# A scan with routing on one Trainium2 core: GpSimd's waits for the residual and for dt move one product ahead, and the token numbers come from a table

## The reference

```python
x_ssm, x_gate = split(x @ in_proj_w.T + in_proj_b)
x_conv = silu(causal_conv4(x_ssm) + conv_b)
Bm, Cm = split(x_conv @ bc_w.T + bc_b)            # 16 states
dt = softplus(x_conv @ dt_w.T + dt_b)
h = h * exp(dt * A) + dt * Bm * x_conv            # step by step over 512 tokens
y = (sum_n h * Cm + x_conv * D) * silu(x_gate)
x = norm(x + (norm(y @ out_w.T + out_b + x) * ln_g + ln_b))
top4 = the 4 best of 8 experts by x @ router_w.T + router_bias, softmax weights
x = norm(x + sum over top4 of weight * expert(x))
```

## Time and profile before

| | |
|---|---|
| time, median of 3 runs | 1290.69 us (1286.31 to 1291.71) |
| time of the profiled execution | 1288.71 us |
| span of the profiled execution | 1286.6 us, so 2.1 us lie around it |
| busy over the span | PE 90%, DVE 82%, ACT 68%, POOL 58% |
| stage 1 | to about 580 us |
| the experts' tiles | from about 580 to 1265 us |
| granted TensorE clock | 0.954 of full speed |

### The profile page before, as it was taken

How to read it: one execution, slowest core, us unless ns; L and a number is a source line. 1 busy time by engine, 2 the same in 40 slices (tenths; PEclk the granted TensorE clock), 3 DMA queues, 4 the chain that set the end, 5 groups by cost and what they waited for, 6 DMA issues and landing times. The chain is left out here.

```text
span 1286.6 us, 17895 instructions
## 1 busy us (share of the span) xinstructions
PE 1153.6 (90%) x5150; PEld 801.9 (62%) x5150; DVE 1053.5 (82%) x1811; ACT 872.4 (68%) x1546; POOL 750.1 (58%) x536
## 2 busy tenths in 40 slices
PE   9879898989898998586979999999999999999960
PEld 4324353535343534255868888888888888888850
DVE  4999999999999999977747777777777777777744
ACT  4675868695959594534647767777677776767745
POOL 0466658888889897976633344433444433444353
PEclk9899999989999998997989999999999999999985
DMA  3543535554545544545856665666665666656638
GB/s 108 213 165 131 182 131 208 175 203 163 195 171 191 187 161 169 212 143 204 283 166 166 156 166 136 160 167 159 167 139 151 166 168 156 155 141 163 166 42 268
DMA packets 69260, 217.21 MB, mean 169 GB/s; under 512 B 7520, under 2 KB 43232, under 8 KB 56288
## 3 DMA queue, kind: packets, MB, share of 16 engines
q1 hardware_dynamic: 33888, 171.61, 37.5%
q0 software_dynamic: 26880, 36.72, 16.5%
q10 hardware_dynamic: 8448, 8.39, 2.0%
HBM read 165.54 MB, written 51.15 MB: 168 GB/s over the span
## 5 line engine op out<-in xcount | busy, mean ns | idle before, releaser
L662 PE MATMUL p_y<-read,small 128*128 128x512 f32 x512 | 252.0, 630 | 54.5 <-POOL read L1312 54.5
L1117 DVE TENSOR_TENSOR_SCAN state<-decay,p_bu 128x512 f32<-128x512 f32 x256 | 297.2, 1202 | 1.7 <-ACT decay L862 1.6
L1640 POOL DMA_INDIRECT total<-o_v,tok x144 | 251.6, 1747 | 39.8 <-issue 39.7
L662 PEld LDWEIGHTS p_y<-read,small 128*128 128x128 f32 x512 | 99.3, 200 | 192.0 <-issue 110.3
L1638 POOL TENSOR_TENSOR scrap<-neg_half 128x1 f32<-128x1 f32 x36 | 22.9, 637 | 314.3 <-ACT o_v L1552 311.8
L520 DVE TENSOR_SCALAR up_v<-up_v 128x512 f32<-128x512 f32 x144 | 69.1, 480 | 144.1 <-ACT up_v L515 139.7
L512 ACT ACTIVATE gate_v<-p_g,bias 128x512 f32<-128x512 f32 x144 | 98.6, 685 | 128.9 <-PE p_up L502 126.8
L862 ACT ACTIVATE decay<-dt,scan_rate 128x511 f32<-128x511 f32 x256 | 162.2, 709 | 10.3 <-DVE state L1117 9.8
L1354 POOL DMA_INDIRECT queues<-rows,index x128 | 129.8, 1014 | 35.0 <-issue 33.0
L1312 POOL TENSOR_TENSOR read<-state,bc 128x1024 f32<-128x1024 f32 x64 | 127.9, 2003 | 37.9 <-DVE p_bu L1108 14.4
L533 ACT ACTIVATE ah<-a_v 128x512 fp32r<-128x512 f32 x144 | 91.3, 634 | 57.9 <-DVE a_v L526 54.8
(11 more groups left out here) (236 smaller groups left out, 2981.5 us busy)
## 6 DMA issues: line engine op xcount, KB each, us to landing
bc<-bc_rows SPq DMA_DIRECT2D x32, 1024.0 KB
first_raw<-in_w_experts SPq DMA_DIRECT2D x19, 1668.0 KB
raw_w<-in_w_experts SPq DMA_DIRECT2D x18, 1668.0 KB
first_wh<-bc_rows SPq DMA_DIRECT2D x16, 1024.0 KB
first_wl<-bc_rows SPq DMA_DIRECT2D x16, 1024.0 KB
first_rows<-queues SPq DMA_DIRECT2D x19, 544.0 KB
xq<-queues SPq DMA_DIRECT2D x18, 544.0 KB
queues<-pad SPq DMA_DIRECT2D x9, 544.0 KB
```

Source lines behind the costliest of these rows:

```text
L662: mm = pe.matmul(p_y[h][:, :], ident[:, :], read[:, t % 4, h, :], start=False, stop=(t == SLOTS - 1))
L1117: dve.tensor_tensor_scan(state[t % 4][:, h, :], decay[(SLOTS * s.n + t) % AHEAD][:, h, :], p_bu[:, h * LEN:(h + 1) * LEN], 0.0, ALU.mult, ...
L1640: pool.indirect_dma_start(total, bass.IndirectOffsetOnAxis(ap=tok[t.p][:, a:a + 1], axis=0), o_v[t.p][:, a, :], None, compute_op=ALU.add). ...
```

## The change

Three things change. (1) POOL's wait for the residual stands ahead of product 7 and not of product 8, its wait for dt ahead of product 11 and not of product 12. (2) The scatters 0 to 6 of a sequence are dealt out anew: 0, 1 and 2 ahead of product 7, 3 ahead of product 9 as before, 4 and 5 ahead of product 11, 6 behind product 14; in round 7 only 0, 1 and 2 move. The second `power` stands ahead of product 11 and not behind it. (3) The constant `token` holds the numbers of all 4096 tokens (32 columns and not 4); ACT copies four columns of it into `rows` ahead of `second_norm`, DVE does so for the last sequence, and the two token steps of `weigh_experts` are gone.

```diff
-    c["token"] = p[:, None] + P * np.arange(TT)[None, :]
+    c["token"] = p[:, None] + P * np.arange(SEQS * TT)[None, :]
...
-                       ("spill", SUBS), ("token", TT), ("ln_g", D), ("ln_b", D), ("b_router", E))
+                       ("spill", SUBS), ("token", SEQS * TT), ("ln_g", D), ("ln_b", D), ("b_router", E))
...
-    ROUTE_STEPS = 12
+    ROUTE_STEPS = 10
...
         def second_norm(r):
             s = r.s.at(-1)
             after(act, s_left, s.n)
+            act.activation(rows[s.p][:, :, COL_TOKEN].bitcast(I32), token[:, TT * s.n:TT * (s.n + 1)], ACT.Copy)
             apply_norm(s, 1, rows[s.p], s_x1)
...
             dve.wait_ge(s_left, s.n)
+            dve.tensor_copy(rows[s.p][:, :, COL_TOKEN].bitcast(I32), token[:, TT * s.n:TT * (s.n + 1)])
             dve.wait_ge(s_last_rstd, 2)
...
-            yield from steps.step(dve.tensor_copy(rows[s.p][:, :, COL_TOKEN].bitcast(I32), token[:, :]))
-            yield from steps.step(dve.tensor_scalar(token[:, :], token[:, :], float(LEN), None, ALU.add))
...
-        BEHIND_READ = (0,)
-        SCATTERS = {9: (1, 2), 10: (3,), 13: (4,)}
-        BEHIND_DRIVE = (5, 6)
-        NEXT_TO_LAST = {9: (1, 2), 10: (3,), 11: (4, 5), 12: (6,)}
+        SCATTERS = {8: (0, 1, 2), 10: (3,), 12: (4, 5)}
+        BEHIND_DRIVE = (6,)
+        NEXT_TO_LAST = {8: (0, 1, 2), 10: (3,), 11: (4, 5), 12: (6,)}
...
-            if r.c and t == 9:
+            if r.c and t == 8:
                 pool.wait_ge(s_residual, r.s.at(-1).n + 1)
-            if r.a and t == 13:
+            if r.a and t == 12:
                 pool.wait_ge(s_dt, r.s.at(1).n + 1)
...
+                if r.c and r.b and t == 12:
+                    power(r.s.at(-1), 1)
                 if r.b:
                     while_scanning(r, t)
...
-                if r.d and r.b and t == 8:
-                    scatter(r.s.at(-2), BEHIND_READ)
...
-                if r.c and r.b and t == 12:
-                    power(r.s.at(-1), 1)
```

## The result

| | before | with the change | ratio, 95% interval |
|---|---|---|---|
| first comparison, median | 1289.7 us | 1277.16 us (1275.62 to 1282.05) | 0.9905 [0.9876, 0.9934] |
| second comparison | 1289.12 us | 1278.31 us | 0.9924 [0.9903, 0.9946] |
| third comparison | 1287.67 us | 1280.18 us | 0.9931 [0.9913, 0.9949] |

The changed kernel is faster by 0.7 to 0.95%. Its first profiled execution is the slowest of the four runs of that comparison, 1282.05 us (span 1280.2); the profiled execution of the second comparison took 1274.84 us (span 1273.0).

The account below looks back on a forecast made before the run. DVE was taken to bound the scans' rounds; 6.55 + 3.1 - 0.5 + 2.35 + 0.3 + 0.85 = 12.65 us off 1288.71 gave 1276.1, set at 1277 us to allow for run scatter; range 1272 to 1283.

Parts of the forecast that it names:

- The residual: DVE's first add of the residual falls to 0.41 us once POOL runs scatters beside it; 6.55 us over rounds 1 to 6.
- dt: `add_log` falls from 1.83 to 1.21 us in rounds 2 to 6; 3.1 us gained.
- The 0.5 taken off for product 10: Deduction because product 10 might still hold `add_log` by up to 0.25 us in the first full rounds.
- Tokens: DVE's two token steps gone: 2.35 us in rounds 2 to 6, 0.3 in round 7, 0.85 behind the scans.
- the sentence that follows product 11 to 347.6: Product 11 ends near 347.6, not 343.5; slot 15's scan needs it at 352, SP's load some 13 us on.
- The rule used for `residual` and `add_log`: A product of POOL holds up a DVE instruction with both inputs in SBUF until the product ends.
- the rule weighed: Whether scatters beside the residual block its add, as the Trainium skill's strict reading says; judged not, nothing charged.
- The prediction's first step: DVE, busy 65.5 of 66.0 us in round 4, sets the pace; shortening its list of a round shortens the round.
- Scatters that hold the adds: Rival: scatters hold the residual and `add_log` as products did; only the tokens' 3.5 us remain, 1285.2 us; chance 0.07.
- PE and ACT as the bound: Rival: PE and ACT set the round, no full round below 66.0 us; gain 6.75 us, 1282 us; chance 0.09.
- The stalled scan: Rival: late product 7 stalls slot 11's scan if POOL pauses between scatters; two pauses give 1301 us; chance 0.04.
- its 0.3: Gain counted in round 7 for the removed token steps, with POOL busy up to the index and through the last product.

## Why the prediction was right, and what in it was not

The time was right: 1277 forecast, medians of 1277.2, 1278.3 and 1280.2 measured, all inside the range. The holds were read rightly, and the scatters freed the adds as said. That the first median lies within 0.2 us of the forecast is luck: single executions of the changed kernel took 1274.84 to 1284.30 us, rounds 1 to 7 gave 8.3 and 9.3 us of the 11.8 that the sum had for them, and what lies ahead of them and behind made up for this or took more away. Point by point:

- *The residual.* 6.55 us forecast, 16.7 - 10.2 = 6.5 measured in the line's busy time. The scatters covered the wait, as said, and the late product 7 did not stall slot 11's scan.
- *dt.* 3.1 us forecast and 3.1 measured. The 0.5 taken off for product 10 was not needed: `add_log` took 1.21 to 1.22 in all rounds, since product 10 ended at 335.9 in round 4 and `add_log` started at 336.16, with 0.25 us to spare.
- *Tokens.* The index follows the weights' step at once. A full round of the change gains 1.84 us and loses 0.21 of `drive`; together that is 2.05 of the forecast 2.09, so the 0.47 is in it. With the tokens alone none of it was. ACT's copy takes 0.19 us.
- *A step that failed* is the sentence that follows product 11 to 347.6 and asks only when slot 15's scan and SP's load need it. Behind product 11 stand products 12 and 13, and in the change they reach the moment when DVE comes to `drive`, which has both inputs in SBUF like the two adds. The rule used for `residual` and `add_log` held for the third such step of the round, and was not asked there. The hold took 0.51 + 1.26 + 0.83 = 2.6 us, nearly all that rounds 1 to 6 lack: 9.25 us against 1.80 + 1.84 + 8.36 = 12.0 without the 0.5. Freeing `drive` gave back 1.5 of it, in rounds 1 and 2; the rest went to `add_log`. A full round was 64.7 us, just outside the forecast 64.4 to 64.6. Some 1.0 of the 1.26 in round 2 come from a cost that the rule weighed left at nothing: it asked whether a scatter holds an add, and not whether an add holds a scatter.
- *The terms do not add as the sum had them.* The prediction's first step, that DVE sets the pace and that what shortens DVE's list of a round shortens the round, fails as long as a step is held. A held step ends when POOL's product ends, and POOL's list from `scale` to `drive` runs without a wait for another engine, from a start that hangs on the gate through PE and ACT: `scale` starts 26.2 us behind the gate of round 4 in before, with the tokens alone and with the residual alone. What DVE saves ahead of a held step is lost in it. Tokens and residual, 8.9 us of the sum over the rounds, gave 0.17% and 0.13% by themselves, with intervals that reach no change, and neither shortened a full round by over 0.1 us. So the sum came out because all parts were made together.
- *Rivals.* Scatters that hold the adds: refuted by the 0.41 us beside two of them. The prediction's evidence for that was thinner than it says, since the compare of 299.07 ran for most of its time in the pause between two scatters (the one ahead ended at 299.14). The next compare is the better one: it ran from 299.64 for 0.42 us, wholly beside the scatter of 299.44. The Trainium skill's page "SBUF — State Buffer", section "Who interferes with whom", has the later of two such instructions blocked for the whole of the other; the traces bear this out for products (an add that starts 0.07 us behind one takes 2.21 us), and for scatters only where the scatter is the later one (1.96 us in round 2). An add that starts behind a scatter isn't blocked (0.41 us). PE and ACT as the bound: not at 66 us; a wait of that kind returns at 64.9, where product 13 is late. Its price in the prediction has a slip: with no full round below 66.0, round 2, which took 66.26, could gain 0.26 and not 1.85, so 5.2 us and not 6.75. The stalled scan: real, at about 3 us more of lag than the change has.
- *Not foreseen beside that.* Round 7 loses its 0.3 and up to 1 us more in two of three profiles, in each of which PE's last sums ran partly at the lower clock level (twelve sums in 7.09 and 7.06 us, 5.90 in the third). The stage behind the scans varies by 6 us between executions of one kernel; why DVE's small plan steps pause there in some executions is open, and no run was made on it.

## What to carry to other kernels

When an instruction is lengthened by another engine's, ask where the other engine's list is anchored: the held step ends when that list says so, and time saved ahead of it is lost in it; here it was worth 0.05 us or less of a full round, and only freeing the last hold paid by itself. After moving a piece of that list, look up what the moved pieces now stand beside, for every instruction of the held kind and not only for those that the change aims at. A wait on the busy engine should have work of its own in front of it: here the order of the scatters gave all of the gain but 1.3 us in round 1, and the waits without it cost 0.6%. Work that is put there can be held by the instruction that it frees, so its start against that instruction is to be looked up too.

## What the runs showed of the hardware that was not expected

A scatter issued by GpSimd and a VectorE add with two SBUF inputs disturb each other in one order only. The add isn't held (0.41 us with two scatters beside it, 0.97 to 2.21 where it met a product of 2.00 us). The scatter is held if it starts inside the add. Over all traces, 28 scatters that started 0.1 to 0.7 us into a 128x1024 add took 1.34 to 1.97 us and ended 0.82 to 0.88 behind the add; 33 that started at most 0.1 us ahead of one took 0.96 to 0.99. GpSimd's own small steps are held by such adds too: the power on 128x4 took 2.03 us beside `dt` and 1.04 without it. TensorE's clock reaches a kernel that VectorE bounds: twelve sums that took 5.90 us at a granted clock of 1.00 took 7.75 at 0.69 in another execution of the same program, and the residual of the round waited 1.6 us more.
